# Late weights packed into four arrays and fetched after the parts are stored, in a four-stage network on one core

## The reference, cut to what matters

```python
for stage in (0, 1, 2, 3):
    xn = layernorm(x)
    s = attention[stage](xn, ...)      # 16 heads of 8 features in stages 0 to 2
    g = silu(feed_forward[stage](xn, ...))
    x = x + s * g
```

## Time and profile before

| | us |
|---|---|
| median of 3 runs | 3964.98 |
| lowest, highest | 3964.82, 3969.65 |
| the profiled execution's own time | 3962.53 |
| its span in the trace | 3960.7 |

### The profile page before, as it was taken

One profiled execution on the slowest core, in us unless ns is written; L12 is line 12 of the kernel. 1 busy time (PEld: TensorE's weight loads), 2 busy tenths in 40 slices (PEclk: granted clock), 3 DMA queues, 4 the chain that ended last, 5 costly groups with the idle time before them and its releaser, 6 DMA issues. The chain is left out here.

```text
span 3960.7 us, 55447 instructions
## 1 busy us (share of the span) xinstructions
PE 3417.7 (86%) x19803; PEld 1783.7 (45%) x19959; DVE 2567.4 (65%) x5513; ACT 1771.5 (45%) x3776; POOL 990.3 (25%) x855
## 2 busy tenths in 40 slices
PE   5888898888988889888988889888898889888877
PEld 2345434444344443444344443444434444444444
DVE  5666765666567665666656665666656666576675
ACT  1454444543444535544344444445354453444424
POOL 3032311332023310333113330233203331133224
PEclk8999999999999999999999999999999999999988
DMA  4100101102011021000110020110200001100130
GB/s 163 33 12 28 39 31 33 36 4 68 2 33 38 1 69 32 12 28 34 36 33 31 8 65 4 33 38 1 69 27 18 28 30 40 33 27 13 61 89 22
DMA packets 82300, 138.66 MB, mean 35 GB/s; under 512 B 10566, under 2 KB 56808, under 8 KB 79588
## 3 DMA queue, kind: packets, MB, share of 16 engines
q1 hardware_dynamic: 75972, 120.91, 9.6%
q10 hardware_dynamic: 3744, 6.61, 0.6%
q0 software_dynamic: 2304, 7.46, 0.5%
HBM read 105.06 MB, written 29.10 MB: 34 GB/s over the span
## 5 line engine op out<-in xcount | busy, mean ns | idle before, releaser
L652 DVE TENSOR_REDUCE nmax<-banks 128x1 f32<-128x512 f32 (+3 forms) x1216 | 760.1, 658 | 391.9 <-PE banks L462 205.2
L572 ACT ACTIVATE probs<-banks 128x512 f32<-128x512 f32 (+3 forms) x1024 | 475.5, 527 | 292.7 <-PE banks L481 204.6
L462 PE MATMUL banks<-ks,qs 72*128 72x512 bf16 (+3 forms) x1536 | 440.8, 332 | 86.4 <-DVE nmax L652 61.0
L481 PE MATMUL banks<-qs,ks 74*128 74x512 bf16 (+3 forms) x1536 | 446.9, 331 | 46.8 <-ACT probs L572 17.2
L113 PE MATMUL banks<-filler,identb 128*128 128x512 bf16 x1632 | 415.9, 383 | 14.8 <-PEq L445 7.6
L462 PEld LDWEIGHTS banks<-ks,qs 72*128 72x128 bf16 x1536 | 140.9, 98 | 371.5 <-DVE nmax L652 214.6
L572 ACT ACTIVATE early<-banks 128x256 f32<-128x256 f32 (+3 forms) x512 | 194.3, 442 | 168.1 <-PE banks L481 166.7
L1518 ACT ACTIVATE probs<-banks,nm 128x192 f32<-128x192 f32 x512 | 172.1, 421 | 206.7 <-DVE nm L1470 206.7
L113 PEld LDWEIGHTS banks<-filler,identb 128*128 128x128 bf16 x1776 | 170.2, 98 | 203.5 <-issue 57.2
L531 PE MATMUL banks<-probs,v 128*32 128x512 f32 (+3 forms) x2048 | 236.2, 533 | 19.1 <-DVE att L639 10.3
L1552 POOL TENSOR_TENSOR probs<-probs,inv 128x768 f32<-128x768 f32 x128 | 187.0, 1466 | 253.6 <-DVE inv L1480 253.6
(11 more groups left out here) (523 smaller groups left out, 6659.3 us busy)
## 6 DMA issues: line engine op xcount, KB each, us to landing
qs<-parts_scratch SPq DMA_DIRECT2D x300, 96.0 KB
ks<-parts_scratch SPq DMA_DIRECT2D x288, 96.0 KB
parts_scratch<-parts SPq DMA_DIRECT2D x50, 384.0 KB, 2.5
shared<-in_w_h SPq DMA_DIRECT2D x17, 1024.0 KB, 7.9
shared<-in_w SPq DMA_DIRECT2D x26, 256.0 KB, 3.9
qs<-max_parts SPq DMA_DIRECT2D x192, 4.0 KB
xn<-in_x SPq DMA_DIRECT2D x9, 256.0 KB, 2.8
factor_scratch<-g SPq DMA_DIRECT2D x8, 256.0 KB, 2.3
```

The lines of the kernel that those rows point to most:

```text
L462: mm = nc.tensor.matmul(K.ps[:, b, i * keys:(i + 1) * keys], K.qs[0:72, 4 * g + j, t * P:(t + 1) * P], K.ks[0:72, 4 * g + j, 0:keys], star ...
L481: mm = nc.tensor.matmul(K.ps[:, b, q0:T], K.ks[0:KR, h, k * P:(k + 1) * P], K.qs[0:KR, h, q0:T], start=True, stop=not on_tensor)
L572: nc.scalar.activation(probs[:, 4 * (q % QUADS) + m % 4, q0:T], K.ps[:, bank("second", m), q0:T], ACT.Exp, scale=scale).then_inc(exped, 1)
L652: nc.vector.tensor_reduce(nmax[:, t, h:h + len(heads)], K.ps[:, n % 2, 0:len(heads) * keys].rearrange("p (j k) -> p j k", k=keys), AX.X, A ...
```

## The change

Four things change, all in the code of the head:

1. The weights of `late` are laid out beforehand in four arrays with one long row per partition: `kept` (4,224 floats, 16.9 KB a row), `second` (1,411, 5.6 KB), `layers` (6,500, 26.0 KB) and `fourth` (2,518, 10.1 KB). Biases are repeated for all partitions. Each array is one DMA; the names that the stages use become slices of four tiles.
2. POOL issues these four once both stores of parts have landed (`K.saved`), no longer once `gates` has.
3. VectorE no longer sets `ks[64:96]`. A constant array of ones, 2 rows of 16 KB, is loaded into rows 72 and 73 by SP as the last of `soon`, and `spread_loads` has no wait for it; SP waits for `soon` at the end of the block as before.
4. The nine copies of transposed fp4 weights become three on VectorE (one of 352 columns, two of 128) and two on ACT (352 and 128), each waiting for the transposes that it needs.

The diff, without the tables of names and the layout of arrays outside the device's time:

```diff
+KEPT = (("w3_up_late", (E3 - NOW, 4 * P)), ("w3_down_late", (E3 - NOW, 2, D)), ("w3_g", (D,)), ("g3_b", (D,)),
+        ("norm3", (D,)))
...
+PACKS = {"kept": KEPT, "second": SECOND, "layers": LAYERS, "fourth": FOURTH}
+def packed(tile, pack):
+    views, o = {}, 0
+    for name, shape in PACKS[pack]:
+        n = int(np.prod(shape))
+        view = tile[:, o:o + n]
...
+        views[name] = view
+        o += n
+    return views
...
+    views = {}
+    for n in ("second", "layers", "fourth"):
+        tile = sb(n, [P, pack_width(n)])
+        views.update(packed(tile, n))
+        late.append((tile[:, :], A[n][:, :]))
+    late.insert(0, (K.kept[:, :], A["kept"][:, :]))
...
+        ones = np.full((2, H * T // 2), 0x3F803F80, np.uint32).view(np.float32)
+        soon.append((K.ks[72:74, :, :].rearrange("p h t -> p (h t)").bitcast(F32),
+                     nc.inline_tensor(ones, name="ones_c").ap()))
...
                 nxt.store_parts(sp)
-                sp.wait_ge(ones_set, 1)
                 spread_loads(nc, K, sp, keys=False)
...
-                act.wait_ge(ones_set, 1)
                 spread_loads(nc, K, act, queries=False)
+                act.wait_ge(turned, 6)
+                nc.scalar.activation(K.w_gu[:, I1:2 * I1], K.ps[:, 1, 0:I1], ACT.Identity).then_inc(copied, 1)
+                act.wait_ge(turned, 8)
+                nc.scalar.activation(K.w_down[:, 1, :], K.ps[:, 3, 0:P], ACT.Identity).then_inc(copied, 1)
...
-                pool.wait_ge(gates_in, 16 * len(gates))
+                pool.wait_ge(K.saved, 32)
                 fetch(pool, late, K.late_landed)
...
-                nc.vector.memset(K.ks[64:96, :, :], 1.0).then_inc(ones_set, 1)
...
-                dve.wait_ge(turned, len(turns))
-                for _, _, ps, dst in turns:
-                    nc.vector.tensor_copy(dst, ps).then_inc(copied, 1)
+                dve.wait_ge(turned, 3)
+                nc.vector.tensor_copy(K.w_gu[:, 0:I1], K.ps[:, 0, 0:I1]).then_inc(copied, 1)
+                for c in (0, 2):
+                    n = min(P, I1 - c * P)
+                    dve.wait_ge(turned, 7 + c)
+                    nc.vector.tensor_copy(K.w_down[0:n, c, :], K.ps[0:n, 2 + c, 0:P]).then_inc(copied, 1)
```

More of the change, by code:

```diff
@@ L2439, in batch_loop @@
     K.s0_3 = whole("s0_3", bc=True, loads=soon)
[L2440 removed]
+    views = {}
[4 more added lines that the diff above has]
+    late.insert(0, (K.kept[:, :], A["kept"][:, :]))
+    K.w1_q, K.w1_k, K.w1_v, K.w1_o = [views[n] for n in ("w1_q", "w1_k", "w1_v", "w1_o")]
     K.w_gu = sb("w_gu", [P, 2 * I1])
@@ L2442, in batch_loop @@
     K.w_down = sb("w_down", [P, 3, D])
[L2443 to L2464, removed]
+    K.w2_q, K.w2_k, K.w2_v, K.w2_ao = [views[n] for n in ("w2_q", "w2_k", "w2_v", "w2_ao")]
+    K.b2_q, K.b2_k, K.rmsw_col = [views[n] for n in ("b2_q", "b2_k", "rmsw_col")]
+    K.b2_v, K.b2_ao, K.rmsw = [views[n] for n in ("b2_v", "b2_ao", "rmsw")]
@@ L2465, in batch_loop @@
+    K.w2_qkv, K.w2_o, K.w2_up, K.b2_up, K.b2_down, K.ln2_g, K.ln2_b, K.w2_down = [
+        [views[f"{n}{L}"] for L in range(2)]
+        for n in ("w2_qkv", "w2_o", "w2_up", "b2_up", "b2_down", "ln2_g", "ln2_b", "w2_down")]
+    up_now, down_now = views["w3_up_now"], views["w3_down_now"]
     K.w3_up = lambda e: up_now[:, e] if e < NOW else K.up_late[:, e - NOW]
     K.w3_down = lambda e: down_now[:, e] if e < NOW else K.down_late[:, e - NOW]
-    K.w3_gate, K.w3_kvq, K.w3_aet = [whole(n) for n in ("w3_gate", "w3_kvq", "w3_aet")]
@@ L2468, in batch_loop @@
-    late.extend([(K.w3_g[:, :], A["w3_g"]), (K.g3_b[:, :], A["g3_b"].partition_broadcast(P)),
-                 (K.norm3[:, :], A["norm3"].partition_broadcast(P))])
-    K.conv_w, K.conv_b, K.b3_aet = whole("conv_w"), whole("conv_b"), whole("b3_aet")
+    K.w3_gate, K.w3_kvq, K.w3_aet = [views[n] for n in ("w3_gate", "w3_kvq", "w3_aet")]
+    K.conv_w, K.conv_b, K.b3_aet = [views[n][0:96, :] for n in ("conv_w", "conv_b", "b3_aet")]
+    K.iota8 = views["iota8"]
     cos, sin = rope_tables()
@@ L2604, in _ @@
                 pe.wait_ge(quantized, 1)
-                for src, n, ps, _ in turns:
+                for src, n, ps in turns:
                     nc.tensor.transpose(ps, src, K.ident[0:n, 0:n]).then_inc(turned, 1)
@@ L3415, in lay_out @@
     t["mem_w"] = c(np.stack([w1.T, w2.T, w2], axis=1))
+    for n in ("w3_up", "w3_down"):
+        w = t.pop(n)
+        t[n + "_now"], t[n + "_late"] = w[:, 0:NOW], w[:, NOW:E3]
+    for L in range(2):
+        w = np.zeros((3 * P, D), np.float32)
+        w[0:HID2] = t[f"w2_down{L}"]
+        t[f"w2_down{L}"] = tiles(w)
+    t["rmsw_col"] = t["rmsw"].reshape(P, 1)
+    t["iota8"] = np.arange(E3, dtype=np.float32)
+    for pack, table in PACKS.items():
+        whole = np.zeros((P, pack_width(pack)), np.float32)
+        o = 0
+        for n, shape in table:
+            a, width = np.asarray(t.pop(n)), int(np.prod(shape))
+            if a.ndim == 1:
+                whole[:, o:o + width] = a
+            else:
+                whole[0:len(a), o:o + width] = a.reshape(len(a), width)
+            o += width
+        t[pack] = whole
     return t
```

30 lines of the change are left out of this document (22 added, 8 removed).

## The result

The changed kernel is slower: 3980.32 us median (3972.63 to 4000.19, 9 runs) against 3964.98 (3961.53 to 3969.65, 9 runs), a ratio of 1.0046 with a 95% interval from 1.0034 to 1.0059.

A forecast was written before the change was run, and what follows sets the result against it. The head was taken to be bound by late stores, then `qs` loads; the first score product would move from 58.49 to 54.5, 4.0 us less, giving a median of 3961.0 us, with a range from 3952 to 3968.

The forecast's parts named there:

- Fewer issues on POOL: Head, GpSimd's issues of late weights: 0 us, as POOL has nothing else to do and the weights end near 60.
- Ones loaded: Head, VectorE: 6.88 us of memset removed, the rest turned into a wait for `consts`; 3.5 us taken as gain.
- Stores land as in the loop: Head, stores of parts: land 2.5 us after issue, at 31.3 instead of 46.67, 15.4 us earlier.
- Group 0 lands at 54.0: Head, first `qs` loads: packets alternate with late-weight rows, 15.0 + 3.8 + 2.4 us after 32.8; product at 54.5, 4.0 us less.
- Slower, by SP's issues: Rival, end of the head's block: a full queue holds SP's last issues; up to 1 us, or 3969.3 total; chance 0.10.
- fp4 copies hidden: Head, copies split over two engines: about 1 us off a path that is not the last, so 0.
- Slices of wide tiles: 0: Loop, operands as slices: same reads and steps, so 0; rival of slower products, 12 us, 3973, chance 0.05.
- The difference of the spans is that of the starts: Loop: a shift of the first score product's start goes through to the end, so the span changes by as much.
- the rule to coalesce small transfers: Head, late weights: packing them gives no gain that counts, as 46 DMAs already ran at 414 GB/s and no engine waits.

The follow-up runs named there:

- e4: Changed kernel, but ScalarE issues the four late arrays behind its loads of `ks`, GpSimd none: median 3963.76 us, first score product at 43.27.
- e3: Kernel before, but GpSimd issues its 46 late loads only after both stores of parts have landed: median 3999.37 us, first score product at 87.70.
- e1: Changed kernel, but GpSimd issues the four arrays once `gates` has landed, as before the change: median 3971.96 us, first score product at 50.84.
- e18: Changed kernel with ScalarE's wait kept, fp4 copies on VectorE alone, late weights issued by SP: median 3967.64 us, first score product at 49.66.
- e16: Kernel before without SP's and ScalarE's waits for the ones ahead of the `qs` and `ks` loads: median 3979.10 us.
- e17: Kernel before without SP's wait for the ones alone, ScalarE's kept: median 3963.01 us.

## Why the prediction was wrong

The forecast was 3961.0 us, and 19.3 us are missing. Two things were not in it.

The step that failed is "*Fewer issues on POOL*: POOL has nothing else to do in the head: 0. SP waits for all late weights before its first use of the row maxima at 88.13; they end near 60: 0." It asked which instruction waits for the weights and found one at 88. The end of the block does too, because they are GpSimd's. The trace of before had it, though no view prints it: GpSimd's DRAIN ends at 50.44, behind the landing of its last load at 48.51, and is hidden there by SP's issues, which end at 56.53. The change moved all of GpSimd's transfers behind the stores, and with them that DRAIN: 67.54. Against the 54.5 forecast the product is 13.5 us late. Of these, 10.6 are the DRAIN (68.05 - 57.4, as estimated under e4); the other 2.9 are SP's held issues, a rival of the prediction that came true underneath. e3 shows the DRAIN by itself, e1 and e4 what the head is without it.

Step by step:

- *Ones loaded*: right in its working, 1.2 us short in size. Layer norm at 3.90, the wait for `consts` of 3.85 us to 11.75. 3.5 us were taken, the stores give 4.67: the tables and casts ended 0.55 us sooner (15.35, the first addition) and the eight additions took 2.1 us, not 2.8.
- *Stores land as in the loop*: right. The loads went at 29.62, 2.56 us behind the end of the stores' issue (27.06), as in the loop.
- *Group 0 lands at 54.0*: right in its mechanism, and hidden. By the trace's own records the last of its 81 packets passed at 51.0 (q1 from 29.6 to 51: 80; to 52: 83). The 3.0 us less come from its first term: eight of the 27 rows and marks of each engine went before 33.0, ahead of nearly all late rows, where the forecast had all 27 take turns. Behind them the rows did so, one by one: rows of `qs` start at 35.07, 35.85 and 36.65, 0.8 us apart, and a row of `kept` with one of `qs` takes 0.81 at the 25.9 GB/s of the prediction. The lines of the queues, 29.6 to 51 and 29.6 to 52:

```profile
q0 software_dynamic: 391, 5.52, 79.7%
...
q1 hardware_dynamic: 80, 0.29, 4.7%
```

```profile
q0 software_dynamic: 410, 5.79, 79.7%
...
q1 hardware_dynamic: 83, 0.30, 4.6%
```

- *Slower, by SP's issues* (0.10): right in kind. The eleventh issue took 6.25 us and the twelfth 13.11, where ten took 0.68. When the eleventh was let go, 99 packets per engine had been issued and 55 / 3 = 18 moved, 81 queued; at the twelfth 108 - 30 = 78. But in the kernel before the twelfth was let go with 108 - 22 = 86 queued (1.75 us), and in e1 it went through in 0.68 us with as many. So the room is not one number: 78 to 86, around the 81 named as the point from which it decides, and the price was not "up to 1 us" but 2.9. SP ended at 56.37; without GpSimd's DRAIN this would have put the product near 57.4 (56.93 + 0.49), 1.1 us before where it was, and the forecast of 54.5 would have been missed by itself. The line of after that answers to the earlier trace rows:

```profile
L382 SPq DMA_DIRECT2D qs<-parts_scratch x12: 675/675/13112, 29.6 to 43.3; - x12
```

- *fp4 copies hidden*: right, 25 us of cover.
- *Slices of wide tiles: 0*: right as far as a trip shows. The short trips of the changed kernel take 464.0 to 464.7 us, those of the kernel before 464.0 to 464.8.
- *The difference of the spans is that of the starts*: wrong. 9.56 of 16.1 us are the start; 6.5 come behind it, and two long trips give 7.1. The second thing missing was that a trip's length has steps of 3.5 us, and that an edit of the head can change how many trips get the longer one. No row of before shows more than one kind of trip, so the range could not have had it from there. In the medians the start leaves 5.8 of 15.3 us, so the term is of like size there, but trips were measured in one execution of each kernel only.

On the Trainium skill, page "DMA: Bandwidth & Descriptors": the rule to coalesce small transfers ("Rules for kernel authors") was weighed against the trace and given nothing. The runs give something for it: 46 loads by GpSimd landed 50.6 us after the first issue (e3, 34.31 to 84.88), four landed 37.4 us after it (29.91 to 67.33); the 46 issues alone took 25.3 us. Issued early, they took 33.9 us (before, 14.61 to 48.51) against 29.3 (e1, 8.51 to 37.83). That is still not a gain for the forecast, as the block's end waits for either.

## What to carry to other kernels

Before you move a transfer behind something, ask not only which instruction reads its data but on whose engine it is issued: here a block ended only when GpSimd's own transfers had landed, while SP's and ScalarE's stayed under way. Here bulk loads that cross a block's end were best on ScalarE, behind what the next stage needs; on SP their issues took 2.75 to 3.15 us each (e18). And when a gain of 15 us shown in the head's timeline doesn't show in the median, look at the lengths of the loop's trips one by one before blaming the edit: here they come in steps, and one idle wait less (e16 against e17) moved the median by 16 us, as much as the whole head.

## What the runs showed of the hardware that I had not expected

- GpSimd's DRAIN waits for the landing of the DMAs it issued: it ends 0.21 us behind the last landing with four loads (67.54 and 67.33; e1 38.04 and 37.83) and 1.93 us behind it in each of the ten traces with 46 loads (before 50.44 and 48.51; e3 86.81 and 84.88). ScalarE's, with 35 us of transfers still to come (e4), took 0.6 us.
- SP's issue is held when 78 to 86 packets per DMA engine are queued: up to 13.11 us for one.
- One DMA of 128 long rows took SP 2.75 to 3.15 us to issue behind its twelve loads of `qs` and `kept` (e18) and ScalarE 0.37 to 0.56 behind its twelve of `ks` (e4). That it is the same hold is likely, not shown.
- A trip of the same instructions takes 464, 467.6 or 471 us, by how long the granted clock is at its lower level in it, and with a satisfied wait on ScalarE outside the loop taken out the long ones became more frequent (five against none in the profiles of e16 and e17, medians 3979.10 against 3963.01).
